# Causal masking of the row maxima moved from matmuls to ScalarE copies and a GpSimd select in an attention kernel on one Trainium2 core

## The chip, the cores and the metric

One core of one Trainium2 chip (trn2). The metric is the device time of one execution in microseconds; several runs of the same kernel are given by their median.

## The reference

The input x has 16 batches of 256 tokens and 256 channels. It passes four residual blocks; only the first is touched by the change:

```
q, k, v = split(layernorm(x) @ Wq.T, Wk.T, Wv.T)      # 16 heads of 16
scores  = q @ k.T / 4, masked: keys after the query get the lowest float
x = x + (softmax(scores) @ v) @ Wo.T
```

After it come a feed-forward block whose weights are splines of control points, a gated linear attention, and the feed-forward block again. All is float32.

## The kernel before

The attention stage (0 to about 370 us) runs over the 16 batches b. A batch has eight steps p; a step handles one pair of heads, which TensorE computes in the two row halves of its array. Each engine has its own program, written out by hand as `period(b, ...)` for that engine; the order of the work on an engine is the order of its program, and semaphores counted per batch (`a_...`, waited for with `upto(a, b, k)`) tie the engines together. Weights and activations are split into a high and a low part, so a projection is three matmuls (lines 419 to 421).

The softmax needs, for each query, the maximum of its allowed scores before the exponentials. So the scores are computed twice. First `scores(b + 1, p)` (line 920), one batch ahead, writes queries on partitions and keys along the row into `pair_b`, [128, 2 heads, 512]: columns 0 to 127 are the second query tile against the first key tile, where every key is allowed, 128 to 383 the two diagonal blocks, and 384 to 511 the block where nothing is allowed. `hide_future` (line 932) then adds -3e38 to the forbidden places of the two diagonal blocks with four small bf16 matmuls on a table `causal_neg` that GpSimd made at the start (lines 733 to 741). VectorE's `maxima` (line 1816) reduces 3 blocks of 128 keys, 768 numbers per partition, to 6 maxima in `mx`, and by that frees `pair_b` for the next pair (semaphore `a_mx`). In the first batch, which nothing precedes, `pair_a` and `pair_b` take turns.

After four pairs `merge_max` (lines 1823, 1824) joins the blocks' maxima, TensorE turns them (`turn_max`, line 939), `split_max` (lines 1830, 1832) splits them into two rows, and SP writes these with four DMAs into the stacked operand `stack` (`max_row`, line 492). Then `shifted(b, p)` (line 951) computes the scores a second time, turned and with the maximum already subtracted, into `pair_a`. ScalarE takes the exponentials (line 1427) into `prob`, GpSimd sets the forbidden ones to zero (`mask`, line 696), and `weigh` (lines 965, 969) multiplies with the values. The half h = 0 of the maxima of batch b + 1 is turned at step 5 of batch b and used at its own step 0; the half h = 1 is turned at step 1 of the batch itself and used at step 4.

Around this the same eight steps carry the other work: the layer norm of batch b + 3 (VectorE `stats` and `normalise`, line 1776, GpSimd `rstd`, line 690), the turn and projections of b + 2 (steps 1, 3 and 5), the values of b + 1 (step 4), and the output of b - 1 (steps 2, 3 and 7). ScalarE copies every result out of its bank (lines 1408 to 1439) and VectorE makes the low halves (1802, 1807, 1850). SP's queue also loads X four batches ahead (line 560) and writes the projected queries and keys into `stack` (line 487). GpSimd makes the spline factors, 24 pieces between step 4 of b = 0 and step 3 of b = 3 (lines 709 to 719), and TensorE and ScalarE turn them in b = 4 to 8. Batches 14 and 15 also start the feed-forward block.

What comes before batch 0's step 0 has its own order: projections of batches 0 and 1, then the eight scores and maxima of batch 0, in two halves with the first half's maxima turned in between. In it ScalarE issues two of the DMAs to `stack` for each half of a batch and two rows of maxima. Where a TensorE wait would be long, `keep_clock` runs matmuls without use.

The chain before the change, as the code has it for one pair:

```
pe.wait_ge(a_mx, upto(a_mx, b, p - both))            # scores: bank free
dve.wait_ge(a_sp, upto(a_sp, b, p + 1))              # maxima: mask added
pe.wait_ge(a_e, upto(a_e, b, p))                     # shifted: exponentials of p - 1 out
pool.wait_ge(a_e, upto(a_e, b, p + 1))               # mask
```

## Time and profile before

| | |
|---|---|
| median of 3 runs | 807.57 us (806.41 to 810.4) |
| profiled execution | 804.9 us |
| its span, first to last instruction | 803.1 us |
| mean granted TensorE clock | 0.983 of full speed |
| attention stage | about the first 370 us |

The profile page lists the busy time of each engine (PE is TensorE, PEld its weight loads, DVE VectorE, ACT ScalarE, POOL GpSimd, SP the sync engine whose queue issues most DMAs). A busy share is a mean over stages; it doesn't tell which wait ends last. In groups and timelines a line names the code line, the operation, out<-in by the program's names with shapes; "x4" is a count, and a bracket with an arrow is the idle time before it and the engine whose work ended that. PE matmuls overlap, so their spacing tells more than their duration. Times from instruction to instruction are read from the starts.

### The profile page before, as it was taken

The numbers are of one execution on the slowest core, as the hardware profiler recorded it, in microseconds if no ns is written. First come the engines' busy times: TensorE is split into PE (matmuls) and PEld (weight loads), VectorE is DVE, ScalarE is ACT, GpSimd is POOL, SyncE is SP. The second block draws the span as 40 slices with busy tenths as digits, with TensorE's granted clock in tenths as the row PEclk, the third lists the DMA queues.
The fourth block names the chain that finished last, engine by engine and source line by source line (L and its number), as shares of the span: only waits on it lengthen the run. The fifth ranks groups of instructions, "written<-read, shape, count | busy, mean of one in ns | idle before, by whom it ended". The sixth has DMA issues, their size and how long they took to land.

```text
span 803.1 us, 19484 instructions
## 1 busy us (share of the span) xinstructions
PE 760.2 (95%) x6874; PEld 657.1 (82%) x6874; DVE 614.9 (77%) x1273; ACT 480.2 (60%) x932; POOL 246.0 (31%) x337
## 2 busy tenths in 40 slices
PE   7789999999999999787999999999999989999998
PEld 6667777777787777565999998899999969999997
DVE  5578877777787887836788877779999757888766
ACT  3145555555555556555676757477888846667653
POOL 5057752222232223231000000246766660000000
PEclk9899999999999999988999999999999998999999
DMA  6866656556686455747766671000024434677741
GB/s 168 115 131 102 100 98 115 87 95 89 87 147 94 99 93 88 161 137 262 239 249 244 243 256 69 1 1 2 2 80 142 171 129 170 217 277 278 284 177 53
DMA packets 70982, 111.47 MB, mean 139 GB/s; under 512 B 7061, under 2 KB 27958, under 8 KB 70854
## 3 DMA queue, kind: packets, MB, share of 16 engines
q1 hardware_dynamic: 68848, 108.47, 50.7%
q10 hardware_dynamic: 2048, 1.88, 1.3%
q8 instruction: 51, 0.84, 0.5%
q14 instruction: 35, 0.29, 0.1%
HBM read 41.82 MB, written 42.81 MB: 105 GB/s over the span
## 4 chain that ended last, share of the span: by engine, by line
PE 72%; DVE 9%; SPq 6%; DMA 5%; ACT 4%; issue 3%; POOL 0%; ACTq 0%; DVEq 0%; POOLq 0%
PE bank L419 12%; PE bank L420 11%; PE bank L421 11%; PE pair_a L951 5%; PE bank L965 3%; PE pair_b L920 3%; SPq L492 3%; DMA stack<-mrow 3%; PE pair_a L1207 3%; PE pair_b L1210 3%; PE bank L1297 3%; DVE inter L2003 3%; PE pair_b L1297 3%; PE pair_a L1262 2%; DVE in_lo L2008 2%
## 5 line engine op out<-in xcount | busy, mean ns | idle before, releaser
L419 PE MATMUL bank<-wd_hi,in_hi 128*128 128x256 f32 x512 | 146.3, 286 | 2.6 <-DVE X L2014 1.7
L1427 ACT ACTIVATE prob<-pair_a 128x768 f32<-128x768 f32 x128 | 103.7, 810 | 70.6 <-PE pair_a L951 69.0
L696 POOL TENSOR_SCALAR_AFFINE_SELECT prob<-prob 128x512 f32<-128x512 f32 x128 | 82.4, 644 | 206.3 <-ACT prob L1427 206.0
L420 PE MATMUL bank<-wd_lo,in_hi 128*128 128x256 f32 x512 | 144.8, 283 | 0.0
L421 PE MATMUL bank<-wd_hi,in_lo 128*128 128x256 f32 x512 | 144.6, 282 | 0.0
L1816 DVE TENSOR_REDUCE mx<-pair_b 128x6 f32<-128x768 f32 x124 | 117.8, 950 | 33.7 <-PE pair_b L932 31.7
L1592 ACT ACTIVATE in_hi<-inter 128x512 fp32r<-128x512 f32 x128 | 80.8, 632 | 94.8 <-DVE inter L2003 90.8
L2008 DVE TENSOR_TENSOR in_lo<-inter,in_hi 128x512 fp32r<-128x512 f32 x128 | 88.3, 690 | 51.8 <-ACT in_hi L1592 50.3
L419 PEld LDWEIGHTS bank<-wd_hi,in_hi 128*128 128x128 f32 x512 | 97.1, 190 | 8.3 <-issue 2.9
L420 PEld LDWEIGHTS bank<-wd_lo,in_hi 128*128 128x128 f32 x512 | 96.9, 189 | 4.9
L421 PEld LDWEIGHTS bank<-wd_hi,in_lo 128*128 128x128 f32 x512 | 97.0, 189 | 0.0
L2003 DVE TENSOR_TENSOR inter<-gact,pair_b 128x512 f32<-128x512 f32 x128 | 87.0, 680 | 5.5 <-PE pair_b L1210 4.4
L951 PE MATMUL pair_a<-stack 50*128 50x256 f32 x512 | 65.4, 332 | 14.4 <-DMA stack<-mrow 10.7
L1584 ACT ACTIVATE gact<-pair_a 128x512 f32<-128x512 f32 x128 | 74.5, 582 | 4.0 <-PE pair_a L1207 3.9
L951 PEld LDWEIGHTS pair_a<-stack 50*128 50x128 f32 x512 | 39.0, 186 | 37.2 <-DMA stack<-mrow 14.2
L920 PE MATMUL pair_b<-stack 48*128 48x256 f32 x496 | 54.4, 296 | 5.4 <-DMA stack<-stage 3.4
L767 POOL TENSOR_TENSOR frs<-fve,half_neg 128x4 f32<-128x4 f32 x16 | 16.1, 1008 | 139.2 <-DVE fve L1982 139.2
L1210 PE MATMUL pair_b<-stk,cst 126*128 126x512 f32 x128 | 53.8, 420 | 1.4 <-DVE inter L2003 1.2
L1207 PE MATMUL pair_a<-stk,cst 126*128 126x512 f32 x128 | 52.6, 411 | 1.3 <-ACT gact L1584 1.3
L1415 ACT ACTIVATE stage<-bank 128x512 fp32r<-128x512 f32 x32 | 19.1, 598 | 49.7 <-PE bank L421 43.8
L965 PE MATMUL bank<-prob,V 128*32 128x256 f32 x512 | 41.8, 399 | 5.2 <-POOL prob L696 5.1
L920 PEld LDWEIGHTS pair_b<-stack 48*128 48x128 f32 x496 | 38.7, 188 | 8.5 <-DMA stack<-stage 3.6
(234 smaller groups left out, 1933.0 us busy)
## 6 DMA issues: line engine op xcount, KB each, us to landing
stk<-fx SPq DMA_DIRECT2D x128, 252.0 KB
stack<-stage SPq DMA_DIRECT2D x184, 128.0 KB, 4.3
fx<-fs SPq DMA_DIRECT2D x32, 512.0 KB, 4.7
fx<-fs SPq DMA_DIRECT2D x32, 256.0 KB, 5.8
fx<-fs SPq DMA_DIRECT2D x16, 504.0 KB
fx<-fs SPq DMA_DIRECT2D x16, 252.0 KB
X<-in_attn_a_x SPq DMA_DIRECT2D x14, 256.0 KB, 5.3
result<-X SPq DMA_DIRECT2D x7, 512.0 KB, 7.1
```

What stands on the lines that cost most here:

```text
L419: pe.matmul(dst, l_hi, r_hi, start=first, stop=False)
L420: pe.matmul(dst, l_hi, r_lo, start=False, stop=False)
L421: return pe.matmul(dst, l_lo, r_hi, start=False, stop=last)
L696: pool.affine_select(out=diag, in_=diag, compare_op=ALU.is_ge, fill=0.0, base=0, pattern=[[0, 2], [0, 2], [1, P]], channel_multiplier=-1). ...
L920: pe.matmul(dst[:, n, at_col:at_col + S], stack[rows, u, h, p % PR, 0, P * t:P * t + P], stack[rows, u, h, p % PR, 1, :], start=(t == 1), ...
L951: i = pe.matmul(pair_a[:, n, at_col:at_col + S], stack[rows, u, h, p % PR, 1, P * t:P * t + P], stack[rows, u, h, p % PR, 0, :], start=Tru ...
L1210: pe.matmul(pair_b[:, m % 2, :], cst[:, 1, m, :], stk[0:NFX, u, m, :], start=True, stop=True).then_inc(f_.upp, 1)
L1427: act.activation(prob[:, p % 4], pair_a[:, :, P:4 * P], ACT.Exp, scale=DK ** -0.5).then_inc(a_e, 1)
L1592: act.activation(in_hi[:, m % LAG, :], inter[:, m % 2, :], ACT.Copy).then_inc(f_.ih, 1)
L1816: dve.tensor_reduce(mx[:, h, :, p % PR, :], src[:, :, 0:3 * P].rearrange("p n (t k) -> p n t k", t=3), AX.X, ALU.max).then_inc(a_mx, 1)
L2003: dve.tensor_tensor(inter[:, m % 2, :], gact[:, m % 2, :], pair_b[:, m % 2, :], ALU.mult).then_inc(f_.up, 1)
L2008: dve.tensor_tensor(in_lo[:, m % LAG, :], inter[:, m % 2, :], in_hi[:, m % LAG, :].bitcast(F32), ALU.subtract).then_inc(f_.il, 1)
```

## The change

The four mask matmuls of a pair are gone, and with them `causal_neg`. `scores` now signals its own last matmul. VectorE reduces only the all-allowed block, 256 numbers per partition, straight from the bank (`seen_maxima`, semaphore `a_mo`). ScalarE then copies the two diagonal blocks, 512 numbers per partition, to SBUF (`copy_diagonal`, `a_dc`), and this copy is what frees the bank for the next `scores`. GpSimd puts -3e38 at the forbidden places of the copy (`mask_scores`, `a_dm`), and VectorE reduces the copy one step later (`diagonal_maxima`, `a_mx`). The copies have two slots; they lie in the end of X (batches 14 and 15, not loaded yet) up to batch 9 and in `spline`, then free, from batch 10 on. The merge of the first half moves from step 3 to step 4, that of the second half from step 7 to step 0 of the next batch. In the first batch ScalarE's and VectorE's orders are rewritten.

```diff
 WDN = D + 4
+SPLINE_FREE = 10
...
         ident16 = sb("ident16", [P, P], BF16)
-        causal_neg = sb("causal_neg", [P, 2, 2, P], BF16)
         half_neg = sb("half_neg", [P, 2 * TB], F32)
...
         flat = spline[:, :, :].rearrange("p r c -> p (r c)")
+        diagonals = (X[:, NT - 4:NT, :], spline[:, 0:4, :])
         prod = flat[:, 0:MT * NF * WIN].rearrange("p (m f w) -> p m f w", m=MT, f=NF)
...
                           mrow[PR * a:PR * a + PR, h, n, :].bitcast(F32)).then_inc(a_md[h], 16)
+
+        def diagonal(b, p):
+
+            return diagonals[b >= SPLINE_FREE][:, 2 * (p % 2):2 * (p % 2) + 2, :]
...
             def period(b, j, u, prev=True, nxt=True, nxt2=True, nxt3=True):
+                if b + 4 == B - 2:
+                    sp.wait_ge(a_mx, upto(a_mx, SPLINE_FREE - 1, NP))
                 if b < B - 4:
...
+            def mask_scores(b, p):
+                pool.wait_ge(a_dc, upto(a_dc, b, p + 1))
+                pool.sem_inc(passed_pool, 1)
+                blocks = diagonal(b, p).rearrange("p n (t k) -> p n t k", t=2)
+                pool.affine_select(out=blocks, in_=blocks, compare_op=ALU.is_ge, fill=NEG, base=0,
+                                   pattern=[[0, 2], [0, 2], [-1, P]], channel_multiplier=1).then_inc(a_dm, 1)
+
             def factor_piece(n):
...
             rstd(1, 1)
-            pool.memset(causal_neg[:, :, :, :], 0.0).then_inc(s_const, 1)
-            pool.wait_ge(s_const, 5)
-            for n in range(2):
-                i = pool.affine_select(out=causal_neg[:, n], in_=causal_neg[:, n], compare_op=ALU.is_ge,
-                                       fill=NEG, base=HALF * n, pattern=[[-HALF, 2], [1, P]],
-                                       channel_multiplier=-1)
-            i.then_inc(s_const, 1)
-            pool.wait_ge(s_const, 6)
+            pool.wait_ge(s_const, 4)
+            pool.wait_ge(a_rs, upto(a_rs, 1, 1))
             ones_rows(1, 0)
...
             pool.memset(zeros[:, :], 0.0).then_inc(s_zero, 1)
+            for p in range(NP):
+                mask_scores(0, p)
...
                     mask(b, p)
+                    if nxt:
+                        mask_scores(b + 1, p)
                     if 4 <= NP * b + p < 28:
...
                     pe.wait_ge(a_stk[h], upto(a_stk[h], b, 16 * N_STACK))
-                pe.wait_ge(a_mx, upto(a_mx, b, p - both))
+                pe.wait_ge(a_dc, upto(a_dc, b, p - both))
                 dst = pair_a if both and p % 2 else pair_b
...
                         rows = slice(HALF * n, HALF * n + K_S)
-                        pe.matmul(dst[:, n, at_col:at_col + S], stack[rows, u, h, p % PR, 0, P * t:P * t + P],
-                                  stack[rows, u, h, p % PR, 1, :], start=(t == 1), stop=False,
-                                  tile_position=(HALF * n, 0))
-                return dst
-
-            def hide_future(dst):
-
-                for half in range(2):
-                    for n in range(2):
-                        rows = slice(HALF * n, HALF * n + HALF)
-                        blocks = dst[:, n, P:3 * P].rearrange("p (b k) -> p b k", b=2)
-                        keys = ident16[rows, rows].rearrange("p (o k) -> p o k", o=1).to_broadcast([HALF, 2, HALF])
-                        i = pe.matmul(blocks[:, :, HALF * half:HALF * half + HALF], causal_neg[rows, n, half, :],
-                                      keys, start=False, stop=half == 1, tile_position=(HALF * n, 0))
+                        i = pe.matmul(dst[:, n, at_col:at_col + S], stack[rows, u, h, p % PR, 0, P * t:P * t + P],
+                                      stack[rows, u, h, p % PR, 1, :], start=True, stop=True,
+                                      tile_position=(HALF * n, 0))
                 i.then_inc(a_sp, 1)
...
             proj_qk(1, 1, 0)
-            pe.wait_ge(s_const, 6)
             pe.wait_ge(s_prep_lo, 4)
...
             for p in range(4):
-                hide_future(scores(0, 0, p, both=True))
+                scores(0, 0, p, both=True)
                 if p == 1:
...
             for p in range(4, NP):
-                hide_future(scores(0, 0, p, both=True))
+                scores(0, 0, p, both=True)
                 if p == 5:
...
                 keep_clock(16, bank_t)
-            pe.wait_ge(a_mx, upto(a_mx, 0, NP))
+            pe.wait_ge(a_dc, upto(a_dc, 0, NP))
...
                     if nxt:
-                        hide_future(scores(b + 1, 1 - u, p))
+                        scores(b + 1, 1 - u, p)
                     if p % 2 == 0 and (p or prev):
...
+            def copy_diagonal(b, p, src=pair_b):
+                act.wait_ge(a_mo, upto(a_mo, b, p + 1))
+                act.wait_ge(a_mx, upto(a_mx, b, p - 1))
+                if b == SPLINE_FREE and p == 0:
+                    act.wait_ge(s_ct, 10)
+                act.activation(diagonal(b, p), src[:, :, P:3 * P], ACT.Copy).then_inc(a_dc, 1)
+
             def copy_o(b, h):
...
             high_weights(3)
-            for h in range(2):
-                copy_qk(1, h, True, (bank_p, bank_o)[h])
-                high_stack(1, h)
+            copy_qk(1, 0, True, bank_p)
+            high_stack(1, 0)
+            for p in range(4):
+                copy_diagonal(0, p, (pair_b, pair_a)[p % 2])
+            copy_qk(1, 1, True, bank_o)
+            high_stack(1, 1)
             act.wait_ge(a_ml, upto(a_ml, 0, 1))
...
                 max_row(act, 0, 0, 1, n)
+            for p in range(4, NP):
+                copy_diagonal(0, p, (pair_b, pair_a)[p % 2])
             high_weights(4)
...
                     exps(b, p)
+                    if nxt:
+                        copy_diagonal(b + 1, p)
                     if b == 0 and p == 1:
...
-            def maxima(b, p, both=False):
+            def seen_maxima(b, p, both=False):
                 dve.wait_ge(a_sp, upto(a_sp, b, p + 1))
...
                     dve.wait_ge(a_m, upto(a_m, b - 1, 2 * (p // 4) + 2))
-                h = p // 4
                 src = pair_a if both and p % 2 else pair_b
-                dve.tensor_reduce(mx[:, h, :, p % PR, :], src[:, :, 0:3 * P].rearrange("p n (t k) -> p n t k", t=3),
+                dve.tensor_reduce(mx[:, p // 4, :, p % PR, 0], src[:, :, 0:P], AX.X, ALU.max).then_inc(a_mo, 1)
+
+            def diagonal_maxima(b, p):
+                dve.wait_ge(a_dm, upto(a_dm, b, p + 1))
+                dve.tensor_reduce(mx[:, p // 4, :, p % PR, 1:3], diagonal(b, p).rearrange("p n (t k) -> p n t k", t=2),
                                   AX.X, ALU.max).then_inc(a_mx, 1)
...
             def merge_max(b, h):
+                dve.wait_ge(a_mo, upto(a_mo, b, 4 * h + 4))
                 dve.wait_ge(a_mx, upto(a_mx, b, 4 * h + 4))
...
             stats(2, 0)
-            maxima(0, 0, both=True)
-            maxima(0, 1, both=True)
-            low_qk(1, 0)
-            maxima(0, 2, both=True)
-            maxima(0, 3, both=True)
+            for p in range(4):
+                seen_maxima(0, p, both=True)
+                if p:
+                    diagonal_maxima(0, p - 1)
+                if p == 1:
+                    low_qk(1, 0)
+            diagonal_maxima(0, 3)
             merge_max(0, 0)
-            maxima(0, 4, both=True)
             split_max(0, 0)
-            maxima(0, 5, both=True)
-            low_qk(1, 1, bank_o)
-            maxima(0, 6, both=True)
-            maxima(0, 7, both=True)
+            for p in range(4, NP):
+                seen_maxima(0, p, both=True)
+                if p > 4:
+                    diagonal_maxima(0, p - 1)
+                if p == 5:
+                    low_qk(1, 1, bank_o)
+            diagonal_maxima(0, NP - 1)
             merge_max(0, 1)
...
                     if nxt:
-                        maxima(b + 1, p)
+                        seen_maxima(b + 1, p)
+                        if p:
+                            diagonal_maxima(b + 1, p - 1)
                         if b == 0 and p == 1:
                             low_gla_weights()
-                        if p == 3:
+                        if p == 4:
                             merge_max(b + 1, 0)
-                        if p == 7:
-                            merge_max(b + 1, 1)
+                    if p == 0 and prev:
+                        diagonal_maxima(b, NP - 1)
+                        merge_max(b, 1)
                     if p == 1:
```

The hunks left out only register the semaphores.

## Rows read from the trace of the kernel before

**Rows 1.** the page, part 1

```profile
PE 760.2 (95%) x6874; PEld 657.1 (82%) x6874; DVE 614.9 (77%) x1273; ACT 480.2 (60%) x932; POOL 246.0 (31%) x337
```

**Rows 2.** groups of the attention stage, 0 to 400 us: busy us, mean ns, idle

```profile
L1816 DVE TENSOR_REDUCE mx<-pair_b 128x6 f32<-128x768 f32 x124 | 117.8, 950 | 33.7 <-PE pair_b L932 31.7
L1427 ACT ACTIVATE prob<-pair_a 128x768 f32<-128x768 f32 x128 | 103.7, 810 | 70.6 <-PE pair_a L951 69.0
L696 POOL TENSOR_SCALAR_AFFINE_SELECT prob<-prob 128x512 f32<-128x512 f32 x128 | 82.4, 644 | 206.3 <-ACT prob L1427 206.0
...
L1807 DVE TENSOR_TENSOR stage<-bank,stage 128x512 fp32r<-128x512 f32 x32 | 21.8, 680 | 13.5 <-ACT stage L1415 13.3
...
L1433 ACT ACTIVATE oT<-bank 128x512 f32<-128x512 f32 x32 | 19.1, 597 | 8.9 <-PE bank L969 8.7
```

**Rows 3.** windows: us, then busy us of each engine, clock, DMA

```profile
60.00:80.00 20.00, 19.55 (x236) 15.17 (x232) 16.15 (x35) 11.26 (x18) 14.75 (x18) 1.00 0.64 101
241.17:261.10 19.93, 19.09 (x228) 14.97 (x229) 15.45 (x34) 10.23 (x15) 5.79 (x9) 1.00 0.65 95
```

**Rows 4.** timeline of TensorE, batch 10: start us, us, instruction

```profile
241.16 0.50 PE L951 MATMUL pair_a<-stack 50*128 50x256 f32 x4
...
241.74 0.28 PE L932 MATMUL pair_b<-ident,causal_neg 64*128 64x128 bf16 x4
241.96 0.64 PE L965 MATMUL bank<-prob,V 128*32 128x256 f32 x8
...
244.39 0.50 PE L951 MATMUL pair_a<-stack 50*128 50x256 f32 x4
...
247.04 0.46 PE L920 MATMUL pair_b<-stack 48*128 48x256 f32 x4
...
258.89 0.48 PE L920 MATMUL pair_b<-stack 48*128 48x256 f32 x4
...
261.10 0.50 PE L951 MATMUL pair_a<-stack 50*128 50x256 f32 x4
```

**Rows 5.** timeline of ScalarE, batch 10, the exponentials of step 1

```profile
243.38 0.80 ACT L1427 ACTIVATE prob<-pair_a 128x768 f32<-128x768 f32 x1
```

**Rows 6.** timeline of VectorE, batch 10

```profile
243.75 0.96 DVE L1816 TENSOR_REDUCE mx<-pair_b 128x6 f32<-128x768 f32 x1 [0.72 <-PE pair_b L932]
...
246.00 0.94 DVE L1816 TENSOR_REDUCE mx<-pair_b 128x6 f32<-128x768 f32 x1
...
257.87 0.94 DVE L1816 TENSOR_REDUCE mx<-pair_b 128x6 f32<-128x768 f32 x1
...
259.35 0.73 DVE L1776 TENSOR_SCALAR xn<-X,mv,rs 128x256 f32<-128x256 f32 x2
```

**Rows 7.** timeline of the SP queue, batch 10

```profile
257.37 2.57 SPq L492 DMA_DIRECT2D stack<-mrow  x4
```

**Rows 8.** timeline of GpSimd and VectorE, 77 to 100 us

```profile
77.37 1.18 DVE L1776 TENSOR_SCALAR xn<-X,mv,rs 128x256 f32<-128x256 f32 x2
...
97.92 1.20 POOL L709 TENSOR_TENSOR spline<-spline,cpw 128x504 f32<-128x504 f32 x1
...
98.31 0.82 DVE L1823 COPY mx<-mx 128x8 f32<-128x8 f32 x1
```

**Rows 9.** timeline of all engines, the first batch

```profile
25.76 1.23 ACTq L487 DMA_DIRECT2D stack<-stage  x2
...
30.73 0.17 DVE L1823 COPY mx<-mx 128x8 f32<-128x8 f32 x1
...
35.18 2.10 ACTq L492 DMA_DIRECT2D stack<-mrow  x2
...
38.38 0.17 DVE L1823 COPY mx<-mx 128x8 f32<-128x8 f32 x1
...
39.45 0.50 PE L951 MATMUL pair_a<-stack 50*128 50x256 f32 x4
...
48.80 0.30 PEld L951 LDWEIGHTS pair_a<-stack 50*128 50x128 f32 x4 [0.21 <-DMA stack<-mrow]
```

More of the change, by code:

```diff
@@ L315, in build @@
         a_mx = counted("a_mx", NP)
+        a_mo = counted("a_mo", NP)
         a_m = counted("a_m", 4)
@@ L320, in build @@
         a_res = counted("a_res", 1)
-        by_dve = [a_bn, a_mv, a_ve, a_xn, a_xl, a_qkl, a_mx, a_m, a_mh, a_ml, a_rd, a_at, a_atl, a_res]
+        by_dve = [a_bn, a_mv, a_ve, a_xn, a_xl, a_qkl, a_mx, a_mo, a_m, a_mh, a_ml, a_rd, a_at, a_atl, a_res]
         a_rs, a_pm = counted("a_rs", 1), counted("a_pm", NP)
-        by_pool = [a_rs, a_pm]
+        a_dm = counted("a_dm", NP)
+        by_pool = [a_rs, a_pm, a_dm]
         a_xh, a_qkh = counted("a_xh", 1), counted("a_qkh", 2)
@@ L328, in build @@
         a_o, a_ath = counted("a_o", 2), counted("a_ath", 1)
-        by_act = [a_xh, a_qkh, a_v, a_e, a_o, a_ath]
+        a_dc = counted("a_dc", NP)
+        by_act = [a_xh, a_qkh, a_v, a_e, a_o, a_ath, a_dc]
         a_xT, a_qkp, a_vp = counted("a_xT", 1), counted("a_qkp", 2), counted("a_vp", 1)
```

## Prediction

> **What bounds the kernel now.** I read the page first: TensorE is busy for 95% of the span, VectorE for 77%, ScalarE 60%, GpSimd 31% [rows 1]. The groups of the attention stage say what the change touches: the reduction of 768 scores (0.950 us), the exponentials (0.810), GpSimd's mask (0.644), a 512-wide copy out of a bank by ScalarE (0.597) and a 512-wide VectorE operation out of a bank (0.680) [rows 2]. In the windows a batch without extra work (b = 10) takes 19.93 us, with TensorE busy 19.09, VectorE 15.45, ScalarE 10.23, GpSimd 5.79; the window 60 to 80, where GpSimd also makes the spline factors, has GpSimd at 14.75 of 20 [rows 3].
>
> By these shares TensorE is the limit, and all it sheds would be gained. The timelines say less. A batch has eight steps; step p of batch b issues shifted(p), scores(p) of batch b+1, the mask matmuls, and some other matmuls. The mask matmuls of step 0 hold TensorE from 241.74 to 241.96, 0.22 us [rows 4]. But three waits stand right behind it. (a) Step 2's shifted needs the exponentials of step 1, which ScalarE began at 243.38, 2.22 us into the batch [rows 5]; from step 0 to step 2 TensorE has no use for time saved. (b) scores(3) starts at 247.04 and scores(7) at 258.89, when the reductions that free pair_b, begun at 246.00 and 257.87, have ended 0.10 and 0.08 us before [rows 4, 6]. (c) The next batch starts at 261.10, 3.73 us after SP began to issue the rows of maxima at 257.37 [rows 4, 7], which is all that transfer takes; this one has no slack at all.
>
> **The parts, for b = 4 to 13.** Removed from TensorE: 8 x 0.22 = 1.76 us a batch.
>
> VectorE: 768 elements in one instruction become 256 from the bank and 512 from the copy. Between the 768 and 512 rows an element costs (0.950 - 0.680) / 256 = 1.05 ns [rows 2], so the first takes 0.41 us and the second 0.68 at most, as from a bank; no row shows a reduction out of SBUF, and between 0.54 (512 x 1.05 ns and nothing fixed) and 0.68 I take 0.65, nearest to the row. The pair costs 1.06 against 0.95: 0.9 us a batch more on VectorE, hidden by its 4.5 us of idle time [rows 3]; if that cover goes, all 0.9 is lost.
>
> ScalarE: 8 copies x 0.60 = 4.8 us a batch, 15.0 of 19.9 busy. Most lie where it waits for TensorE, but the copy of step 0 and the one of copy_o stand before exponentials 1, so (a) stays where it is, 0.04 us later by my count. GpSimd: 8 x 0.64 = 5.1 us, 10.9 busy; hidden, except below.
>
> **Release of pair_b**, the step that decides. Before: reduction 0.95, then scores(p+1), with about 0.1 us of slower weight loading behind it, 1.1 in all. After: first reduction 0.41, start of ScalarE 0.07 (estimate, as after other VectorE releases), copy 0.60, start of TensorE 0.21 (exponentials 1 end at 244.18, step 2 follows at 244.39 [rows 4, 5]), and the same 0.1: 1.4. It starts 0.22 earlier. So each step in which the release decides loses 0.3 and gets 0.22 back. In steps 0 to 3 two releases follow one another: scores(3) comes 0.4 later, of which the missing mask matmuls return 0.22, and step 4 starts 0.2 later. Steps 4 and 5 have TensorE work of 2.4 us and more and gain 0.44. In step 7 of a batch like b = 10, scores(7) gains nothing (the 0.44 goes into the longer release, since on VectorE the low half of the projection, itself behind the split of the maxima, stands before the first reduction), and the mask matmuls behind it give 0.22. SP's issue, 0.44 earlier, allows that. Sum for b = 9 to 13: 0.2 - 0.44 + 0.2 = about 0, range -0.5 to +0.5 each. For b = 4 to 8 TensorE has the factor work in step 6, which covers the release, so steps 4 to 7 give 0.88, less 0.2: 0.65 each, 3.2 us in all.
>
> **A port.** While GpSimd ran its 1.20 us product from 97.92, the 8-element copy in merge_max, 0.17 otherwise [rows 9], took from 98.31 to 99.13 [rows 8]; the two normalisations at 77.37, next to GpSimd's work, took 1.18 instead of the 0.73 of 259.35 [rows 6, 8]. VectorE's SBUF copies thus wait for GpSimd to finish. The new mask of step 6 falls on the normalisations, which stand before the first reduction of step 7, and up to 0.4 us can be lost there; I take 0.1 for b = 9 to 13, 0.5 us in all. The Trainium skill, page "SBUF — State Buffer", section "Who interferes with whom", has this as an exclusive lock of one port pair for copies and tensor_scalar, the other side fully blocked, while a reduction never contends; by its rule every batch would lose the rest of a mask at the normalisations, up to 0.64, which would make the 0.5 us 3.2.
>
> **b = 1 to 3: GpSimd.** In the window 60 to 80 it works 14.75 us [rows 3]; 8 masks more make 19.9, the length of the batch. It lags, the weighing of the probabilities and the second reductions wait for masks, and nothing is gained; I count 0.4 us lost for b = 1 and 2, nothing for b = 3.
>
> **The first batch.** Before, its first four reductions ended with the merge at 30.73, the second four at 38.38, and batch 0 started at 39.45 [rows 9]. Now each pair also goes through ScalarE and GpSimd, 0.60 + 0.64 + 0.65 and handoffs, about 2.1 us behind the first reduction, with two buffers. ScalarE's two DMA issues end at 26.99 [rows 9], then come the copies, the last of the four at about 31.5; merge at 33.0 instead of 30.7. For the second four ScalarE must first issue the two rows of maxima, 2.10 us before, from about 34.7; the copies begin at 36.8, the last ends at 41.3, the merge comes at 42.8 instead of 38.4. Batch 0 itself can start at about 41.6, when the last copy is out. Behind the merge stand the weights' low halves and the normalisation, then the rows for step 4, which landed at 48.80 [rows 9]. So 4.4 us later, with nothing behind to win it back. Bounds: 2 (the rows of maxima issue in 0.6 each) to 7 (the clock drops in the longer waits). I take 4.5. The removed constants and their masks on GpSimd lie before its idle time: 0.
>
> **The end.** Batch 14's rows of maxima go through an SP queue full of other loads, and batch 15 has no scores: 0. Diagonal 7 and its merge move into the next batch's step 0; they end before step 1's turn of the maxima. The X load of b = 10 waits for reductions long done: 0.
>
> Sum: 4.5 + 0.8 + 0.5 - 3.2 = +2.6 on the profiled execution's 804.9 (span 803.1): 807.5. The median of the runs, 807.57, lies 2.7 above the profiled one: 810.
>
> **Rivals.** About 4 us (0.5%) is what a measurement here can tell from no change.
>
> 1. *TensorE keeps the pace* (faster, 0.25). If handoffs are shorter than I take them (the ends that I call releases are ends of recorded latency), all 1.76 us of ten batches come back, less 4.5 of the start: -13, median 794.5. For it: TensorE is 19.09 of 19.93 busy. Against: (a), (b), (c). Half of it gives 801.
>
> 2. *The release is longer than 1.4* (slower, 0.36). ScalarE's queue is in order: a copy that waits for VectorE holds the exponentials, or the copies for the projections, behind it. Each 0.1 us over 1.4 costs 0.1 at three releases (steps 2, 3, 7) of 13 batches, 3.9 us. It decides from 0.04 over, where my +2.6 passes 4; with 0.2 over it gives 818.
>
> 3. *GpSimd binds the first batches harder*: the weighing waits for a mask at steps 0 and 2, where the steps are shortest, and 1 us is lost in each of three batches. For it: 19.9 of 20 us. Against: steps 3 to 5 are long enough to catch up. 812; its chance is part of the forecast's, whose side of 4 us it stays within or near.
>
> My forecast, no measurable change, has 0.39; its own range is 804 to 812. The whole range takes half of rival 1's gain and rival 2 with 0.25 over: 800 to 821.
>
> **What would show it.** Batch 0 starts near 41.6 instead of 39.45, and its step 4 near 53 instead of 48.8. The plain batches near 240 unchanged within 0.5 us, with TensorE's busy time 1.7 less and its idle time before scores' matmuls put down to ScalarE's diagonal copy; b = 4 to 8 shorter by 0.6. ScalarE near 15 of 19.5, and GpSimd near 19 of 20 in 60 to 100. Wrong if the plain batches shorten by over 0.5 (rival 1) or grow by as much (rival 2), or if batch 0 starts before 40.5.

## Result and profile after

| | before | after |
|---|---|---|
| median | 808.99 us (806.41 to 810.56, 4 runs) | 821.84 us (818.38 to 823.01, 4 runs) |
| profiled execution, its span | 804.9, 803.1 us | 823.01, 820.9 us |
| mean granted clock | 0.983 | 0.96 |

Ratio 1.0155, 95% interval 1.0109 to 1.0201: 12.8 us slower, where no measurable change was forecast; 821.84 is 0.8 us above the top of the forecast's range. Measured once more (e16 below) the change took 818.24 us, which is inside that range, with a ratio of 1.0130 [1.0092, 1.0168]; the intervals overlap, and the size is read as 10 to 13 us. One execution of e4 (1157.77 us) and one of e16 (3873.43 us) lie far outside the others and don't count in the ratios.

From the page of after: the shares, and the row of the clock in 40 slices of 20.5 us.

```profile
PE 763.5 (93%) x6362; PEld 652.4 (79%) x6362; DVE 631.0 (77%) x1401; ACT 547.3 (67%) x1060; POOL 324.0 (39%) x462
...
PEclk9767999999999999978999999999999998999999
```

TensorE's share falls by two points [rows 1], since its busy time grows by 3.3 us while the span grows by 17.8; in slices 2 to 4 the granted clock is well below full. The groups of the attention stage in after, answering to [rows 2]:

```profile
L1836 DVE TENSOR_REDUCE mx<-X 128x4 f32<-128x512 f32 x80 | 54.0, 675 | 8.5 <-POOL X L713 8.5
L1832 DVE TENSOR_REDUCE mx<-pair_b 128x2 f32<-128x256 f32 x124 | 51.8, 418 | 18.2 <-PE pair_b L935 17.2
L713 POOL TENSOR_SCALAR_AFFINE_SELECT X<-X 128x512 f32<-128x512 f32 x80 | 51.0, 639 | 33.9 <-ACT X L1438 33.5
L1438 ACT ACTIVATE X<-pair_b 128x512 f32<-128x512 f32 x76 | 45.5, 598 | 39.8 <-DVE mx L1832 34.3 <-issue 4.9
```

The prices of the single operations are those of the prediction. What is new is the 34.3 us that ScalarE stands still in front of its copies until VectorE's first reduction is out.

Windows of after: two early ones, and the plain batch b = 11 (columns: length, busy time of each engine, granted clock, DMA share, GB/s), against [rows 3].

```profile
40.00:60.00 20.00, 16.61 (x137) 12.78 (x136) 13.69 (x38) 11.27 (x22) 7.72 (x13) 0.67 0.42 110
60.00:80.00 20.00, 17.91 (x143) 12.81 (x141) 13.09 (x29) 10.75 (x16) 15.60 (x20) 0.67 0.62 88
...
256.11:275.60 19.49, 18.70 (x198) 14.11 (x198) 16.26 (x42) 14.27 (x24) 10.88 (x17) 1.00 0.68 98
```

**Where the time went.** SP begins to issue the rows of maxima of the first half of batch b about 3.7 us before b starts, so these issues (from SP's timeline) cut the span into batches. In us:

| kernel | b=1 | b=2 | b=3 | b=5 | b=10 | b=15 | span |
|---|---|---|---|---|---|---|---|
| before | 55.65 | 75.06 | 94.61 | 133.97 | 237.43 | 334.18 | 803.1 |
| after | 66.02 | 88.91 | 110.10 | 151.29 | 252.36 | 349.14 | 820.9 |
| e16, after again | 63.42 | 86.12 | 107.33 | 148.22 | 249.33 | 346.14 | 815.1 |
| e1, batch 0 old | 58.23 | 79.95 | 101.10 | 140.88 | 240.87 | 339.39 | 806.9 |
| e2, batches 0 to 4 old | 55.40 | 74.78 | 94.33 | 133.81 | 234.52 | 332.16 | 803.1 |
| e5, batches 0 to 4, 14, 15 old | 57.97 | 77.40 | 96.95 | 135.92 | 237.45 | 334.33 | 802.4 |
| e10, e1 without selects in 1 to 4 | 58.24 | 77.92 | 97.75 | 136.75 | 237.98 | 336.10 | 807.0 |
| e11, e1 with them set aside | 56.36 | 79.10 | 98.98 | 138.58 | 238.41 | 335.32 | 807.6 |
| e13, one reduction first | 62.37 | 84.22 | 105.31 | 146.60 | 246.43 | 342.99 | 814.4 |
| e15, idle matmuls | 63.16 | 84.77 | 105.97 | 146.81 | 246.80 | 343.49 | 809.9 |
| e6, before with selects in 0 to 3 | 57.58 | 81.17 | 101.77 | 141.87 | 244.92 | 341.44 | 809.0 |
| e8, before with selects in 4 to 8 | 55.90 | 77.65 | 97.20 | 136.55 | 239.93 | 336.44 | 808.2 |

At b = 5 the two profiles of the change are 17.3 and 14.3 us late; from there to b = 15 they win back 2.4 and 2.3. The whole loss is made in the first five batches, and 7.8 to 10.4 of it ahead of batch 1. The rest of the program, behind b = 15, then differs by 2.8 and by under 0.1 us: the two readings of the same kernel don't share it.

A single profile shows where time goes, not whether 2 us are real. Two rows of the table say how far unchanged code varies. Kernels e2 and e5 are the same up to batch 12, and their b = 1 lie 2.6 us apart. And e8 is the kernel before until batch 4, yet its batch 1 takes 21.75 us instead of 19.41, and the rest behind b = 15 takes the same 471.8 us as in after. Against e8 the change is 14.7 and 11.7 us late at b = 5. TensorE at the start of batch 1 in e8, and its window, against [rows 3]:

```profile
59.65 0.80 PE L962 MATMUL pair_a<-stack 50*128 50x256 f32 x4 [1.62 <-DMA stack<-mrow]
...
67.95 0.50 PE L962 MATMUL pair_a<-stack 50*128 50x256 f32 x4
...
60.00:80.00 20.00, 19.85 (x216) 14.89 (x214) 14.14 (x30) 10.80 (x17) 12.97 (x16) 0.84 0.60 95
```

and the same two matmuls in the kernel before:

```profile
59.40 0.50 PE L951 MATMUL pair_a<-stack 50*128 50x256 f32 x4 [1.63 <-DMA stack<-mrow]
...
64.95 0.50 PE L951 MATMUL pair_a<-stack 50*128 50x256 f32 x4
```

The same steps 0 to 3 take 8.30 us at a granted clock of 0.59 and 5.55 us at 1.00. So a stretch at the lower clock level in batch 1 is not the change's own: it comes in some executions of the kernel before too, and costs 2.3 us of the batch there.

Batch 0 and the start of batch 1 in after, TensorE's timeline, against [rows 9]; the line at 261.97 is from a plain batch:

```profile
43.83 0.51 PE L955 MATMUL pair_a<-stack 50*128 50x256 f32 x4
...
45.24 0.50 PE L955 MATMUL pair_a<-stack 50*128 50x256 f32 x4 [0.67 <-ACT prob L1430]
47.47 0.50 PE L935 MATMUL pair_b<-stack 48*128 48x256 f32 x4 [1.73 <-ACT X L1438]
...
49.01 0.50 PE L955 MATMUL pair_a<-stack 50*128 50x256 f32 x4
...
53.05 0.80 PE L935 MATMUL pair_b<-stack 48*128 48x256 f32 x4 [0.99 <-ACT X L1438]
...
56.63 0.79 PE L955 MATMUL pair_a<-stack 50*128 50x256 f32 x4
...
69.77 0.69 PE L955 MATMUL pair_a<-stack 50*128 50x256 f32 x4 [1.66 <-DMA stack<-mrow]
...
261.97 0.50 PE L935 MATMUL pair_b<-stack 48*128 48x256 f32 x4
```

ScalarE's timeline of after:

```profile
35.52 2.09 ACTq L496 DMA_DIRECT2D stack<-mrow  x2
37.72 0.60 ACT L1438 ACTIVATE X<-pair_b 128x512 f32<-128x512 f32 x1 [4.93 <-issue]
...
41.78 0.60 ACT L1438 ACTIVATE X<-pair_a 128x512 f32<-128x512 f32 x1 [0.32 <-DVE mx L1832]
...
46.82 0.60 ACT L1438 ACTIVATE X<-pair_b 128x512 f32<-128x512 f32 x1 [1.64 <-DVE mx L1832]
...
261.32 0.60 ACT L1438 ACTIVATE spline<-pair_b 128x512 f32<-128x512 f32 x1 [0.49 <-DVE mx L1832]
```

VectorE's timeline of after:

```profile
44.05 0.17 DVE L1844 COPY mx<-mx 128x8 f32<-128x8 f32 x1
44.13 0.16 DVE L1845 TENSOR_TENSOR mx<-mx 128x8 f32<-128x8 f32 x1
44.21 0.68 DVE L1799 TENSOR_TENSOR wog_lo<-bank,wog_hi 128x512 fp32r<-128x512 f32 x1
44.81 0.68 DVE L1799 TENSOR_TENSOR wig_lo<-bank,wig_hi 128x512 fp32r<-128x512 f32 x1
45.41 1.04 DVE L1793 TENSOR_SCALAR xn<-X,mv,rs 128x256 f32<-128x256 f32 x2
46.38 0.41 DVE L1832 TENSOR_REDUCE mx<-pair_b 128x2 f32<-128x256 f32 x1
...
260.88 0.40 DVE L1832 TENSOR_REDUCE mx<-pair_b 128x2 f32<-128x256 f32 x1
...
273.88 0.83 DVE L1793 TENSOR_SCALAR xn<-X,mv,rs 128x256 f32<-128x256 f32 x2
```

Batch 0 starts at 43.83 instead of 39.45. The merge, before 1.07 us ahead of that start, is now 0.22 behind it, and VectorE's low halves and normalisation follow it, so the first reduction of batch 1's scores (their matmuls start at 44.17 and last 0.40) begins only at 46.38. Then come the copy (46.82) and the next scores (47.47, after a wait of 1.73). Behind this wait and the one at 53.05 the same operations show the durations of the lower clock level, 1.2 GHz (0.79 to 0.80 us for four score matmuls, elsewhere 0.40 to 0.50), and batch 0 is 25.9 us long instead of 19.95.

### The profile page after: what moved, and what is told of

The parts are those of the page before. It is cut to its first block, busy times and chain, and to the rows that moved or that the text cites. A ratio compares the mean times of both kernels' runs of the same rounds, so it can differ in the third digit from the quotient of the medians.

```text
span 820.9 us, 19226 instructions
## 1 busy us (share of the span) xinstructions
PE 763.5 (93%) x6362; PEld 652.4 (79%) x6362; DVE 631.0 (77%) x1401; ACT 547.3 (67%) x1060; POOL 324.0 (39%) x462
## 4 chain that ended last, share of the span: by engine, by line
PE 43%; DVE 7%; ACT 2%; DMA 2%; issue 1%; SPq 1%; POOL 0%; DVEq 0%; ACTq 0%; POOLq 0%
PE bank L423 8%; PE bank L424 8%; PE bank L425 8%; PE pair_b L1213 3%; PE pair_a L1210 3%; DVE inter L2031 3%; PE bank L1300 3%; PE pair_b L1300 3%; PE pair_a L1265 2%; DVE in_lo L2036 2%; ACT in_hi L1609 2%; PE bank L1177 1%; DMA stack<-mrow 1%; PE pair_a L425 1%; PE pair_a L423 1%
## 5 line engine op out<-in xcount | busy, mean ns | idle before, releaser
L955 PE MATMUL pair_a<-stack 50*128 50x256 f32 x512 | 67.6, 342 | 19.0 <-DMA stack<-mrow 13.6
L1438 ACT ACTIVATE X<-pair_b 128x512 f32<-128x512 f32 x76 | 45.5, 598 | 39.8 <-DVE mx L1832 34.3
L935 PE MATMUL pair_b<-stack 48*128 48x256 f32 x496 | 57.8, 310 | 10.4 <-ACT X L1438 8.5
L1832 DVE TENSOR_REDUCE mx<-pair_b 128x2 f32<-128x256 f32 x124 | 51.8, 418 | 18.2 <-PE pair_b L935 17.2
L713 POOL TENSOR_SCALAR_AFFINE_SELECT X<-X 128x512 f32<-128x512 f32 x80 | 51.0, 639 | 33.9 <-ACT X L1438 33.5
L1836 DVE TENSOR_REDUCE mx<-X 128x4 f32<-128x512 f32 x80 | 54.0, 675 | 8.5 <-POOL X L713 8.5
L935 PEld LDWEIGHTS pair_b<-stack 48*128 48x128 f32 x496 | 40.4, 195 | 18.7 <-ACT X L1438 10.0
```

The source lines that it names most:

```text
L935: i = pe.matmul(dst[:, n, at_col:at_col + S], stack[rows, u, h, p % PR, 0, P * t:P * t + P], stack[rows, u, h, p % PR, 1, :], start=True, ...
L955: i = pe.matmul(pair_a[:, n, at_col:at_col + S], stack[rows, u, h, p % PR, 1, P * t:P * t + P], stack[rows, u, h, p % PR, 0, :], start=Tru ...
```

## The experiments

All ratios are against the kernel before in the same comparison. "Old" means as in the kernel before: mask matmuls, one 768-wide reduction, no copy, no select. The lines shown are cuts of each edit.

**e1: batch 0 old.** With the old orders of the first batch:

```diff
+OLD = (0,)
...
 def copy_diagonal(b, p, src=pair_b):
+    if not new(b):
+        return
...
+                if not new(b):
+                    dve.tensor_reduce(mx[:, p // 4, :, p % PR, :],
+                                      src[:, :, 0:3 * P].rearrange("p n (t k) -> p n t k", t=3),
+                                      AX.X, ALU.max).then_inc(a_mx, 1)
+                    return
```

> The changed kernel, but batch 0 masks and reduces its scores as before (mask matmuls, one reduction of 768) in the old order of the first batch; batches 1 to 15 keep the new way. Theory A, the loss is made in the first batch (its chain through ScalarE and GpSimd, and the TensorE clock that falls in the waits) and not in each batch: 10 to 14 us of the 12.8 come back, 808 to 812 us. Rival B, the longer release of pair_b costs 0.9 us in each of 13 batches: about 1 us comes back, 820 to 822 us.

Measured: 808.75 us, 1.0018 [0.9988, 1.0049]. As the first theory expected. By the ratios, 9 to 11 us of the loss (against e16 and after) hang on the way that batch 0's maxima are taken, and a loss in every batch is out.

**e2: batches 0 to 4 old** (against e1).

```diff
-OLD = (0,)
+OLD = (0, 1, 2, 3, 4)
```

> Batches 0 to 4 the old way, 5 to 15 the new. Theory A: batches 1 to 3 had GpSimd full of spline factors and masks, so 1 to 4 us more than with batch 0 alone come back, 806 to 809 us. Theory B: 5 of 13 batches' losses come back, 816 to 818 us.

Measured: 803.46 us, 0.9941 [0.9913, 0.9969]: faster than both kernels, and below what either theory expected. Against e1 that is another 5.3 us by the medians and 6.2 by the ratios, so batches 1 to 4 lose as well, and batches 5 to 15 win some 5 us. Windows of e2: the early clock is full.

```profile
40.00:60.00 20.00, 16.34 (x201) 12.53 (x198) 15.49 (x39) 9.87 (x19) 10.45 (x13) 1.00 0.63 132
60.00:80.00 20.00, 19.64 (x236) 15.23 (x236) 16.15 (x34) 11.34 (x18) 14.54 (x17) 1.00 0.62 102
```

**e5: batches 14 and 15 old as well** (against e2), to see whether the end loses.

```diff
-OLD = (0, 1, 2, 3, 4)
+OLD = (0, 1, 2, 3, 4, 14, 15)
```

> Batches 0 to 4, 14 and 15 the old way, only 5 to 13 the new. With batches 0 to 4 old the run took 803.5 us and its profile lost 2.6 us in the last two batches, where ScalarE also normalises for the feed-forward block. If that is the diagonal copies' doing, 1.5 to 3 us come back: 800.5 to 802 us, faster than both kernels. If it is the DMA queue's own irregularity: 803 to 804 us.

Measured: 802.64 us, 0.9939 [0.9908, 0.997], the same as e2, and between the two expectations. No loss at the end is shown.

**e4: the kernel before, only without the mask matmuls** (no masking before the maxima).

```diff
-                        hide_future(scores(b + 1, 1 - u, p))
+                        scores(b + 1, 1 - u, p)
```

> The kernel before without its mask matmuls and with nothing in their place; it leaves out the masking of the scores before the maxima, so the maxima are taken over forbidden keys too. If TensorE sets the pace of every step: 128 x 0.22 = 28 us less, 781 us. By my three waits (exponentials, reduction, rows of maxima) only 0.8 us a plain batch and 1.3 us one of batches 4 to 8: 10 to 16 us less, 793 to 799 us.

Measured: 802.33 us, 0.993 [0.9901, 0.996]. All 0.22 us a step that the change can save are worth 5.3 us by the medians (3 to 8 by the interval), with nothing put in their place. That refutes the 28 us, but it is also less than the 10 to 16 that the three waits were expected to leave.

**e3: TensorE kept busy in the waits of the first batch and batch 0's step 1.**

```diff
                 if p == 1:
-                    keep_clock(8)
+                    keep_clock(24)
...
+            keep_clock(24)
             turn_max(0, 0)
...
                 if p == 5:
-                    keep_clock(8)
+                    keep_clock(40)
...
+                    if b == 0 and p == 1:
+                        keep_clock(24, bank_t)
```

> The changed kernel with more keep_clock matmuls in the waits of the first batch (24 instead of 8, 24 new ones before the turn of the maxima, 40 instead of 8, 24 new ones in step 1 of batch 0), nothing else. If the fallen clock makes part of the loss: batch 0 still starts near 43.8 us, but at full clock its step 4 comes 2 to 3 us earlier and batch 1 is shorter, 815 to 819 us in all. If only the order of the chain counts: 821 to 823 us.

Measured: 818.3 us, 1.0135 [1.0093, 1.0176]: inside its expectation of 815 to 819, but not to be told from the change measured again (e16, 1.0130).

**e7: ScalarE's two rows of maxima behind its last four copies.**

```diff
-            act.wait_ge(a_ml, upto(a_ml, 0, 1))
-            for n in range(2):
-                max_row(act, 0, 0, 1, n)
             for p in range(4, NP):
                 copy_diagonal(0, p, (pair_b, pair_a)[p % 2])
+            act.wait_ge(a_ml, upto(a_ml, 0, 1))
+            for n in range(2):
+                max_row(act, 0, 0, 1, n)
```

> The changed kernel; in the first batch ScalarE issues the two rows of maxima behind its last four diagonal copies instead of ahead of them. If the in-order wait for the split and the issues (copies from 37.7 us on) are the chain of the second half: batch 0 starts 1.5 to 2.5 us earlier than 43.8 and the whole takes 817 to 820 us. If another link holds it (the low half on VectorE, the masks): 821 to 823 us.

Measured: 818.35 us, 1.0131 [1.0096, 1.0166]. That is inside the expected 817 to 820, but it can't be told from e16, and batch 0 did not start earlier as expected. In its profile the last copy starts at 39.95 instead of 41.78, but batch 0 starts only at 45.15; ScalarE issues its rows from 39.95 on, 4.4 us later than in after, and that batch 0 waits for them is likely but not shown.

**e9: the edits of e3 and e7 together.**

> The changed kernel with both edits that each gave 3.5 us: TensorE kept busy in the waits of the first batch, and ScalarE's two rows of maxima issued behind its last four diagonal copies. If the clock and the order of ScalarE's queue are two separate terms of the first batch's loss, their gains add: 821.8 - 3.5 - 3.5 = 815 us (814 to 816). If they are one term (the later rows only cost because the clock falls in the wait for them), the second edit gives little on top of the first: 817.5 to 818.5.

Measured: 825.64 us, 1.0234 [1.0204, 1.0264]. Outside both expectations. So the two gains of 3.5 us read off e3 and e7 were not to be trusted. Its profile is of the fastest execution (821.06 us) and doesn't show where the others lost more. The next four runs share one comparison.

**e13: one reduction first.**

```diff
             merge_max(0, 1)
+            seen_maxima(1, 0)
             low_weights(4)
...
-                        seen_maxima(b + 1, p)
+                        if b or p:
+                            seen_maxima(b + 1, p)
```

> The changed kernel with one VectorE instruction moved: the first reduction of batch 1's scores (step 0 of batch 0) stands ahead of the low halves of two weights and a normalisation, which in the trace of the change hold it from 44.7 to 46.4 us and with it ScalarE's copy and the next scores matmul. Theory V: VectorE's queue behind the late merge costs 1.3 to 2.5 us of batch 0's 6 extra: 819.5 to 820.5 where the change measures 821.8, and batch 0 is 24 to 25 us long instead of 26. Rival C (the clock alone sets batch 0's length, and what is won at step 1 is waited away): 821 to 822.5.

**e14: e13 and e7.**

> The same, with ScalarE's two rows of maxima issued behind its last four diagonal copies (alone 818.4 us). Theory V: the two waits follow one another, so they add: 816 to 817.5. Rival: 818 to 819.

**e15: e3 again.**

> The run with TensorE kept busy in the first batch's waits, once more, since it gave 818.3 where the same idle matmuls on top of the later rows gave 825.6. If the clock in the first batch is a term of its own, again 3 to 4 us under the change on this chip; if its effect was chance or moves the low stretch to another place, within 1.5 us of the change.

**e16: the change again.**

> The changed kernel itself, once more, as the base for the other three on this chip: 821.8 us, ratio 1.0155, within 1.5 us.

Measured: e13 817.36 us, 1.0114 [1.0082, 1.0146]; e14 818.1, 1.0117 [1.0086, 1.0147]; e15 816.51, 1.0112 [1.0079, 1.0145]; e16 818.24, 1.0130 [1.0092, 1.0168]. VectorE's timeline of e13 shows the reduction where it was wanted, and what it displaced:

```profile
44.76 0.43 DVE L1832 TENSOR_REDUCE mx<-pair_b 128x2 f32<-128x256 f32 x1 [0.24 <-PE pair_b L935]
45.10 0.68 DVE L1799 TENSOR_TENSOR wog_lo<-bank,wog_hi 128x512 fp32r<-128x512 f32 x1
...
46.30 1.04 DVE L1793 TENSOR_SCALAR xn<-X,mv,rs 128x256 f32<-128x256 f32 x2
```

From step 0 to step 2 of batch 0 it takes 4.07 us (43.98 to 48.05) where after and e16 take 5.18: the wait behind VectorE's queue is real and 1.1 us long. In total time neither e13 (0.9 us under e16) nor e14 nor e15 can be told from the change. Of the expectations only the rival's for e14 (818 to 819) came true: e13 fell below both, e15 between them, and e16 is 3.6 us under the 821.8 expected. Repairs of single links don't win back what leaving out the chain does (e1).

**e12: e1 with 16 idle matmuls in step 1 of batches 0 to 2.**

```diff
                     shifted(b, u, p)
+                    if b < 3 and p == 1:
+                        keep_clock(16, bank_t)
```

> Batch 0 masked and reduced the old way, batches 1 to 15 as in the change, with 16 idle matmuls on TensorE in step 1 of batches 0 to 2, where it waits for the exponentials of step 1. Without them the kernel measured 808.8 us. If the clock that falls in the short steps of the first batches is what the later chain costs, 804 to 807 us; if the copies in the release cost at full clock as well, 808 to 810 us.

Measured: 811.23 us, 1.0029 [1.0008, 1.0051], above both expectations, and nothing gained over e1's 1.0018. Yet the idle matmuls did raise the granted clock: 0.91 in each of the windows 40 to 60 and 60 to 80, against 0.74 and 0.83 in e1. It is the same with e15: a mean granted clock of 0.976 over its executions against 0.964 in e16, and a time that can't be told from it. Idle matmuls are no remedy; that they take the time themselves is likely, not shown.

**e6 and e8: the load on GpSimd alone.** The kernel before, with one more select of 128x512 per step on idle memory, in batches 0 to 3 (e6, shown) or 4 to 8 (e8).

```diff
                     mask(b, p)
+                    if 0 <= b < 4:
+                        pool.wait_ge(s_idle, 1 + NP * (b - 0) + p)
+                        blocks = idle.rearrange("p n (t k) -> p n t k", t=2)
+                        pool.affine_select(out=blocks, in_=blocks, compare_op=ALU.is_ge,
...
```

> The kernel before, with one more select of 128x512 on GpSimd behind each mask of batches 0 to 3 (on idle memory, its result used by nobody): GpSimd's load of the changed kernel in these batches without ScalarE's copies and without the longer release. If GpSimd's full queue makes the 5 to 7 us that batches 1 to 4 lose: 812 to 815 us. If the longer release or ScalarE makes them: 807.5 to 809 us.

> As e6_pool_early, but the extra selects stand in batches 4 to 8, where GpSimd makes no factors and is busy for under 6 of 20 us. If only a full queue counts: 807.5 to 808.5 us. If the selects disturb VectorE through the shared port wherever they stand: 809 to 811 us.

Measured: e6 810.24 us, 1.0015 [0.999, 1.0039]; e8 807.23, 0.9992 [0.9964, 1.002]. By the intervals the load alone costs at most some 3 us early, and nothing that can be measured later; e6 lies between its two expectations. Its profile shows that it isn't free: batches 2 and 3 take 20.60 and 20.37 us there, against 19.55 and 19.63 before. In batch 2 TensorE waits 0.9 us for the reductions that free `pair_b`. VectorE's two normalisations stand ahead of the first of them, and take 1.65 us next to GpSimd's work, where before they took 1.18 [rows 8]:

```profile
83.48 1.65 DVE L1787 TENSOR_SCALAR xn<-X,mv,rs 128x256 f32<-128x256 f32 x2
85.05 0.94 DVE L1827 TENSOR_REDUCE mx<-pair_b 128x6 f32<-128x768 f32 x1
...
86.14 0.50 PE L931 MATMUL pair_b<-stack 48*128 48x256 f32 x4 [0.46 <-DVE mx L1827]
```

**e10 and e11: which part of batches 1 to 4.** Both are e1, without masking before the maxima in batches 1 to 4: e10 leaves the select out, e11 makes it on idle memory, where nobody waits for it.

```diff
 def mask_scores(b, p):
-    if not new(b):
+    if not masked(b):
         return
...
-                dve.wait_ge(a_dm, upto_new(a_dm, b, p + 1))
+                if masked(b):
+                    dve.wait_ge(a_dm, upto_masked(b, p + 1))
+                else:
+                    dve.wait_ge(a_dc, upto_new(a_dc, b, p + 1))
```

> Batch 0 masked and reduced the old way; batches 1 to 4 with ScalarE's copies and the second reductions out of the copy, but with no select by GpSimd (the masking before their maxima is left out, so those maxima also see future keys); batches 5 to 15 as in the change. The kernel with the select in them measured 808.8 us, the one with these batches masked the old way 803.5. Theory P, it is the select in the chain on a GpSimd that is full with the spline factors: 803 to 804.5 us. Rival R, it is the copy in the release of pair_b (short steps without other TensorE work, half clock behind the waits): 807.5 to 809 us.

> As the run before, but GpSimd makes a select of the same size per step of batches 1 to 4 on idle memory, so its load is that of the change and no reduction waits for it (the masking before the maxima of these batches is left out). If the load on GpSimd is what costs (the weighing of the probabilities waits behind the selects), about 2 us or more over the run without selects: 806 to 809. If only the chain through GpSimd costs, equal to the run without selects, within 1 us.

Measured: e10 805.44 us, 0.9973 [0.9953, 0.9993], between theory and rival; e11 808.5, 0.9991 [0.9965, 1.0016]. Of the 0.0077 between e1 and e2, 0.0045 go with the selects and 0.0032 with the copies and second reductions; the first is just outside what the intervals allow for chance, the second just inside (e1 and e2 were measured in another comparison than e10). e11 lies between and can't be told from either. By the table, the issues for b = 1 to 5 span 78.5 us in e10, as before (78.3), 82.65 in e1 and 82.2 in e11. Batch 2's own piece, from its issue to that of b = 3, shows the two ways apart: 21.15 us in e1, 21.19 in after, 19.88 in e11, 19.83 in e10, 19.55 before. In these kernels, then, the select costs in batch 2 only where it stands in the chain (1.3 us). With the old 768-wide reductions the same load out of the chain did cost about 1 us in that batch (e6). The waits of TensorE in that batch of after:

```profile
PE bank L969 <- POOL prob L706: 0.9, 1, 0.9
PE pair_b L935 <- ACT X L1438: 0.7, 1, 0.7
```

and in e11:

```profile
PE pair_b L976 <- ACT X L1492: 0.6, 1, 0.6
```

GpSimd's timeline of after in that batch has no gap: the mask of the probabilities that `weigh` waits for (98.75 to 99.38) stands behind a select and a sum of the spline factors.

```profile
96.53 0.65 POOL L706 TENSOR_SCALAR_AFFINE_SELECT prob<-prob 128x512 f32<-128x512 f32 x1
97.14 0.64 POOL L713 TENSOR_SCALAR_AFFINE_SELECT X<-X 128x512 f32<-128x512 f32 x1
97.74 1.05 POOL L730 TENSOR_TENSOR spline<-spline 128x504 f32<-128x504 f32 x1
98.75 0.63 POOL L706 TENSOR_SCALAR_AFFINE_SELECT prob<-prob 128x512 f32<-128x512 f32 x1
```

Batch 1's piece is 22.89 us in after, 22.70 in e16, 21.72 in e1 and 22.74 in e11, but 19.68 in e10. That piece can't tell the parts from each other, since unchanged code takes 19.41 (before) or 21.75 (e8) here. In after TensorE goes from its step 0 to its step 3 in 9.41 us (69.77 to 79.18; before 59.40 to 64.95, 5.55) with one wait of 0.39 and its matmuls at the durations of the lower level: 3.9 us longer, and e8 shows that the clock alone costs 2.75 in the same steps. The windows 60 to 80 have the granted clock at 0.67 in after, 0.74 in e16, 0.83 in e1, 0.75 in e11, 0.91 in e10 and 0.84 in e8.

## Why the prediction was wrong

It forecast no measurable change, and the kernel became slower; the mechanism of its slower rival isn't what happened either. The steps that failed are two terms of its sum: 4.5 us for the first batch, where 7.8 to 10.4 were lost ahead of batch 1, and 0.8 for batches 1 to 3, where some 6 were lost in 1 to 4. By its own steps, with after and e16 as two readings:

- **The first batch, start of batch 0: the kind of delay right, its links too early.** The 4.4 us of the prediction are the delay of the second merge (42.8 instead of 38.4); batch 0 itself was named for 41.6, 2.2 later than before. Measured were 5.7 us for the merge (44.05), and 4.4 and 4.7 us for the start of batch 0 (43.83 and 44.13 instead of 39.45). That the 4.5 of the sum meets the delay of the start is luck. The links came later one by one: fourth copy out at 32.2 instead of 31.5, first merge at 33.9 instead of 33.0, ScalarE's issue of the rows at 35.5 instead of 34.7 (2.09 us long, as predicted), last copy out at 42.4 instead of 41.3. The start was counted 0.3 us behind that copy, where TensorE began 1.45 behind it, as it had begun 1.1 behind the last reduction before.
- **"With nothing behind to win it back": the step that failed.** The sum took the delay once and gave batch 0 its old length. It is 25.9 us in after and 23.1 in e16, against 19.95: 3.2 to 6.0 us more. The prediction itself said that the low halves and the normalisation stand behind the merge, but followed them only to step 4. They also hold the first reduction of batch 1's scores, and now the copy behind it (1.1 us of it shown by e13). Step 4 came at 56.63, predicted near 53. The rest of it stands beside the lower clock level behind these waits, which the prediction had only in its upper bound of 7. The total ahead of batch 1 is 7.8 to 10.4, over that bound; how much of it is the clock's is open.
- **b = 1 to 3, GpSimd: the second failed term.** Predicted 0.8 for b = 1 and 2 and nothing for b = 3. Pieces 1 to 4 lose 6.9 and 6.5 us (in after 3.5, 1.6, 0.7 and 1.1), and 4.6 and 4.2 against e8; the ratios of e1 and e2 give 6.2. The place was right, rival 3's, and so was part of its mechanism, the weighing that waits for a mask in batch 2. The price of 0.8 wasn't: the chain through GpSimd costs 1.3 in batch 2 (e1 against e11), and in batch 1 of after the steps 0 to 3 take 3.9 longer, of which the lower clock level costs 2.75 in e8 without any of the change. The predicted 19.9 of 20 us in 60 to 100 was not seen in after (15.60 and 16.38, as all came later); e1 has 17.48 and 18.00.
- **b = 4 to 8, 0.65 each: half right.** From b = 5 to b = 9 the issues of after and e16 are 81.7 us apart, before 83.5: 0.45 a batch. Batch 4 lost 1.1 and 0.8 instead; why isn't known.
- **Release of pair_b: too long, and too much made of it.** Predicted 1.29 us from the first reduction's start to the scores matmul and 0.1 of slower loading behind. Measured 1.09 (260.88, 261.32, 261.97), before 1.04 [rows 4, 6]. The start of TensorE behind ScalarE's copy takes 0.05 (261.92 to 261.97), where 0.21 had been carried over from the exponentials. So the plain batches gain: 0.60, 0.45, 0.02, 0.37 and 0.38 for b = 9 to 13 by the issues (in e16 each within 0.05). Predicted was 0. Rival 2, which needed a longer release, is out.
- **TensorE's pace: right in direction.** Waits (a) to (c) hold back what TensorE sheds, and more than was counted: leaving the masks out altogether gives 5.3 us (e4), so rival 1's -13 was not there. The sign named for it failed: TensorE's busy time in a plain batch was to fall by 1.7 us and fell by 0.39 (18.70 in b = 11, against 19.09 in b = 10 before).
- **ScalarE near 15 of 19.5:** 14.27 of 19.49. **The diagonal reduction:** 0.675 for the predicted 0.65. **The seen one:** 0.418 for 0.41.
- **The port, 0.1 a batch: right in plain batches.** The two normalisations take 0.83 us there, 0.73 before. In batch 0 they take 1.04 (45.41), in e6 1.74 beside a product of GpSimd. By the rule of the Trainium skill, page "SBUF — State Buffer", section "Who interferes with whom", each would have lost the rest of a mask. The trace of e6 agrees (1.01 us lost, 0.94 of the product left). In the plain batches of after it doesn't: GpSimd's select from 273.61 has 0.37 left when they start at 273.88, and they lose 0.10; there the measurement decides.

```profile
103.50 1.19 POOL L713 TENSOR_TENSOR spline<-spline,cpw 128x504 f32<-128x504 f32 x1
103.75 1.74 DVE L1787 TENSOR_SCALAR xn<-X,mv,rs 128x256 f32<-128x256 f32 x2
...
273.61 0.64 POOL L713 TENSOR_SCALAR_AFFINE_SELECT spline<-spline 128x512 f32<-128x512 f32 x1 [0.59 <-ACT spline L1438]
```

- **The end, 0: not settled.** Piece 14 takes 20.57 us in after and e16, before 19.32, so 1.25 are lost there (e1 and e2 have the same form there and take 22.11 and 21.89); but giving batches 14 and 15 their old form (e5) gained nothing that can be measured over e2.

So, by the profiles: about 8 to 10 us lost ahead of batch 1, 6.5 to 7 in batches 1 to 4 (4 to 5 against e8), 2.3 won in 5 to 14 (3.6 in 5 to 13, 1.25 lost again in 14). By the ratios of e1 and e2: 9 to 11 lost by batch 0's form, 6 by that of 1 to 4, 5 won by the rest. **Shown** is the division by batches (e1, e2, and two profiles of the change), and that the same change pays when it is left out of batches 0 to 4 (e2, e5). The select's share in batches 1 to 4 is shown for batch 2 by the traces, and only barely in total time (e10). **Only argued** is how much of batch 0 is the clock. For batch 1 e8 gives the price of a low stretch, 2.3 us of the batch, but since the kernel before has such stretches too, only part of it can be charged to the change; and where idle matmuls raised the granted clock with the chain left in, the time didn't come back (e12, e15). **Open:** why e9 was slower than the change, and batch 4.

## What to carry to other kernels

Price a longer chain where the pipeline fills, apart from where it runs full: here the same edit won some 0.4 us in each plain batch and lost 12 to 17 in batches 0 to 4. When something starts late, follow every instruction queued behind it on its engine to the first one that someone else waits for, and ask what TensorE does in that gap. If the gain is in the middle, use the new form there alone (e2: 0.9941). Don't read effects of 3 us from four executions, and before a loss in one stage of a profile is charged to an edit, compare that stage in two profiles of unchanged code.

## What the runs showed of the hardware

- In the early batches the lower of TensorE's two clock levels (1.2 instead of 2.4 GHz) came behind short waits: the stretches from 49 to 63 (granted clock 0.52) and from 69 to 80 (0.54) in after stand behind waits of 1.73 and 1.66 us, and TensorE was busy for 13.0 of 14 and 9.8 of 11 us in them. Such a wait doesn't decide it alone: behind one of 1.63 us the kernel before stayed at 1.00, and behind one of 1.62 us the same code in e8 ran at 0.59 for 8.30 us.
- What the level costs: steps 0 to 3 of batch 1, the same matmuls, took 5.55 us at 1.00 (before) and 8.30 at 0.59 (e8).
- The two normalisations on VectorE took 0.73 us in a plain batch before, 0.83 beside the last 0.37 us of a select of GpSimd, and 1.74 beside a product (e6).
- The start of TensorE behind a ScalarE copy took 0.05 us; behind ScalarE's exponentials 0.21 [rows 4, 5].
- A 512-wide reduction out of SBUF takes 0.675 us, as long as an operation out of a bank [rows 2].
